# Softmax weights turned in 32x32 blocks: all pairs instead of every second, through one SBUF exchange

## What is computed

```python
q, k, v = (Q @ Wq + bq), (K @ Wk + bk), (V @ Wv + bv)        # layer 0, heads of 64; K = V = context
scores = einsum('bhqd,bhkd->bhqk', q, k) * scale
attn = softmax(where(attn_mask, -1e9, scores))
out = layernorm(einsum('bhqk,bhkd->bhqd', attn, v) @ Wo + bo + Q) * gamma + beta
...
x = layernorm(tgt + self_attention(tgt, tgt_mask) @ o_w)      # layer 1, heads of 16
x = layernorm(x + cross_attention(x, memory) @ co_w)
x = layernorm(x + relu(x @ lin1_w) @ lin2_w)
```

## Time and profile before

| | us |
|---|---|
| median of three runs | 1821.75 |
| the profiled execution | 1826.15 |
| its span | 1824.3 |
| PE / DVE / ACT / POOL busy | 1719.5 / 1269.6 / 1190.3 / 990.9 |
| DMA traffic | 324.12 MB in 227521 packets |

### The profile page before, as it was taken

One profiled execution on the slowest core, in us unless ns is written; L12 is line 12 of the kernel. 1 busy time (PEld: TensorE's weight loads), 2 busy tenths in 40 slices (PEclk: granted clock), 3 DMA queues, 4 the chain that ended last, 5 costly groups with the idle time before them and its releaser, 6 DMA issues.

```text
span 1824.3 us, 36986 instructions
## 1 busy us (share of the span) xinstructions
PE 1719.5 (94%) x11328; PEld 1287.7 (71%) x11328; DVE 1269.6 (70%) x4778; ACT 1190.3 (65%) x3985; POOL 990.9 (54%) x1030
## 2 busy tenths in 40 slices
PE   7999999999999999999999999999999999998887
PEld 5776677777777677777777777677777777776556
DVE  3465667786868668686776868678686867667763
ACT  3364766667676666767666676766667677566752
POOL 3252655657465464746556474555657565455742
PEclk9999999999999999999999999999999999998899
DMA  7432327585766758576585757658575766613010
GB/s 167 143 106 84 107 67 230 172 273 161 238 204 200 245 170 272 161 244 206 178 266 181 249 159 236 209 181 280 173 251 163 226 223 182 202 59 139 30 58 12
DMA packets 227521, 324.12 MB, mean 178 GB/s; under 512 B 31744, under 2 KB 196352, under 8 KB 219136
## 3 DMA queue, kind: packets, MB, share of 16 engines
q1 hardware_dynamic: 224208, 321.75, 55.5%
q10 hardware_dynamic: 3120, 0.01, 0.1%
HBM read 170.69 MB, written 151.00 MB: 176 GB/s over the span
## 4 chain that ended last, share of the span: by engine, by line
PE 77%; DVE 6%; DMA 5%; ACT 5%; SPq 5%; issue 2%; POOL 0%; POOLq 0%; DVEq 0%
PE ps_g L681 45%; PE ps_t L824 10%; PE ps_t L847 8%; PE ps_s L800 8%; ACT prob L930 3%; PE ps_av L800 3%; DMA prob_b<-p_kept 3%; PE ps_av L847 3%; DVE prob L1105 2%; DMA p_kept<-blocks 2%; SPq L593 1%; PE ps_g L687 1%; DVE res_ln L1081 1%; DVE prob_b L1136 1%; SPq L576 1%
## 5 line engine op out<-in xcount | busy, mean ns | idle before, releaser
L1229 POOL TENSOR_TENSOR prob<-prob,recip 128x512 f32<-128x512 f32 x768 | 788.4, 1049 | 670.5 <-DVE recip L1115 670.4
L930 ACT ACTIVATE prob<-prob,ext 128x256 f32<-128x256 f32 x1536 | 757.2, 499 | 11.7 <-DVE ext L1105 11.5
L940 ACT ACTIVATE prob_t<-ps_t 128x512 f32<-128x512 f32 x384 | 226.3, 594 | 398.1 <-PE ps_t L824 397.3
L824 PE MATMUL ps_t<-ident,prob 128*128 128x128 f32 x1920 | 304.6, 283 | 7.6 <-DVE prob_b L1136 5.4
L930 ACT ACTIVATION_READ_ACCUMULATOR prob<-prob,ext 128x1 f32 x1536 | 295.5, 192 | 0.0
L824 PEld LDWEIGHTS ps_t<-ident,prob 128*128 128x128 f32 x1920 | 216.9, 142 | 94.2 <-issue 51.6
L1105 DVE CUSTOM_DVE_ANT_0 prob<-ps_s,mask_a 128x256 f32<-128x256 f32 x392 | 145.3, 421 | 88.3 <-PE ps_s L800 70.6
L1127 DVE STREAM_TRANSPOSE blocks<-prob 128x512 f32<-128x512 f32 x288 | 183.9, 676 | 3.2 <-POOL prob L1229 2.3
L1105 DVE CUSTOM_DVE_ANT_0 prob<-ps_s,zero 128x256 f32<-128x256 f32 x392 | 144.4, 418 | 45.3 <-PE ps_av L800 37.3
L1105 DVE CUSTOM_DVE_ANT_0 prob<-ps_s,mask_b 128x256 f32<-128x256 f32 x368 | 135.9, 417 | 24.5 <-PE ps_s L800 14.8
L800 PE MATMUL ps_s<-k_ctx,q 64*128 64x256 f32 x784 | 144.8, 402 | 7.3 <-DVE ext L1105 3.0
(11 more groups left out here) (116 smaller groups left out, 2980.9 us busy)
## 6 DMA issues: line engine op xcount, KB each, us to landing
p_kept<-blocks SPq DMA_DIRECT2D x576, 128.0 KB, 2.4
prob_b<-p_kept SPq DMA_DIRECT2D x144, 512.0 KB, 3.4
k_parts_C<-k_hl SPq DMA_DIRECT2D x64, 256.0 KB, 3.1
k_parts_B<-k_hl SPq DMA_DIRECT2D x64, 256.0 KB, 3.1
q_parts_B<-q_hl SPq DMA_DIRECT2D x64, 256.0 KB, 3.5
k_B<-k_parts_B SPq DMA_DIRECT2D x16, 1024.0 KB, 7.6
q_B<-q_parts_B SPq DMA_DIRECT2D x16, 1024.0 KB, 7.7
q_parts_C<-k_hl SPq DMA_DIRECT2D x64, 256.0 KB, 4.7
```

The costliest lines, as they stand in the source:

```text
L824: last = nc.tensor.transpose(two(ps_t[e])[:, kt, qt * P:(qt + 1) * P], src[:, e, qt, kt * P:(kt + 1) * P], ident[:, :])
L930: last = nc.scalar.activation(tile, tile, ACT.Exp, bias=ext[:, slot, e, t:t + 1], scale=-1.0, accum_out=sums[:, slot, e, t:t + 1])
L940: nc.scalar.activation(prob_t[:, e], two(ps_t[e]), ACT.Copy).then_inc(copied_second, 1)
L1229: nc.gpsimd.tensor_tensor(rows, rows, recip[:, slot, e].unsqueeze(2) .to_broadcast([P, TT, TOK]), ALU.mult).then_inc(normed[s], 1)
```

## The change

- The odd pairs are turned on DVE too, in all bodies, and with one instruction of 128x1024 a pair. `T0`, `T1`, `L`, `turn`, `evac_turned` (on DVE and ACT) and `prob_t` are gone, and so is `p_kept`.
- `exchange` takes the place of `spill` and `load_back`: SP issues four transfers of 128 KB from `blocks` straight into `prob_b` for each pair, in the place in which it was turned. `prob_b` holds three quads (`T_RING`), `blocks` two (`B_RING`), `prob` three pairs (`P_RING`, from four). `turn_blocks` waits, for the even pair of a quad, until both pairs of the quad two before have landed; `exchange` until the quad three before was weighed.
- The exchange puts key r*4+g on the partition where the token's own order would have g*32+r. So scores have their key columns in that order: the host gives `ctx_keys` (and both masks) with permuted columns, a new input tile `c_k` feeds the key projections, and `keys_out` reads `x1_t` in that order for `ks`.
- `LAG` is 4 instead of 3: `weigh` comes five places behind the odd pair's scores.
- The banks freed: scores have four of their own (`ps_s`), `weigh` has `ps_av`; PE may start a pair's scores when the pair two before has been masked.
- B's keys and both queries are spread from SBUF to SBUF, eight issues of 128 KB each, without DRAM; the queries' on ACT, in two halves. C's keys still go through DRAM.
- ACT takes `v` instead of DVE. `x` is loaded straight into `res["ln0"]`, to which POOL adds the bias in place. The jobs stand at other places of the list.
- Weights and biases of layer 1 are arranged on the host and come in a few large transfers; POOL's `sort_weights` is gone.

```diff
-P_RING = 4
-LAG, BLOCKS = 3, 2
-BLOCKED = {(s, q) for s in "ABC" for q in range(QUADS)}
+P_RING, B_RING, T_RING = 3, 2, 3
+LAG, BLOCKS = 4, 2
-DVE_JOBS = {"q": 4, "v": 4, "kc": 1, "wo": 1,
+DVE_JOBS = {"q": 4, "kc": 1, "wo": 1,
-ACT_JOBS = {"k": 4, "vc": 1, "x1T": 1, "x2T": 1, "x3T": 1, "h": 3}
+ACT_JOBS = {"k": 4, "v": 4, "vc": 1, "x1T": 1, "x2T": 1, "x3T": 1, "h": 3}
...
             zip("AAABBCACBBCC", (0, 1, 2, 0, 1, 0, 3, 1, 2, 3, 2, 3)) for j in range(2)]
...
+        ("A", 0): [job("k", 2)],
+        ("A", 1): late + [job("ks")],
+        ("A", 2): [job("qs"), dma("k", "B"), ln("ln1")],
+        ("A", 3): [job("x2T"), job("q", 2), dma("q0", "B")],
+        ("A", 4): [job("qc"), dma("q1", "B")],
+        ("A", 5): [job("oc"), job("vs")],
+        ("B", 0): [ln("ln2"), io("value_c"), dma("q0", "C")],
+        ("B", 1): [job("x3T"), job("v", 2), dma("q1", "C"), res("res3", 0), res("res3", 1)],
+        ("B", 2): [job("h", 0)],
+        ("B", 3): [job("hd"), job("q", 3), res("res2", 0), res("res2", 1)],
+        ("C", 0): [job("k", 3), res("res1", 0)],
+        ("C", 1): [job("h", 1), job("h", 2), io("x_columns")],
+        ("A", 6): [job("v", 3), res("res1", 1)],
+        ("A", 7): [half("y")],
+        ("C", 2): [job("y"), io("x_in")],
+        ("C", 3): [io("mask_in"), job("kc"), job("vc")],
+        ("B", 4): [job("q", 0, "x")] * closed + [res("res0", 0)],
+        ("B", 5): [job("q", 1, "x")] * closed + [io("save_c"), io("c_columns"), ln("ln3")],
+        ("B", 6): [],
+        ("B", 7): [half("wo")] * closed + [io("store")],
+        ("C", 4): [job("wo")] * closed,
+        ("C", 5): [job("k", 0, "x"), job("v", 0, "x")] * closed,
+        ("C", 6): [job("k", 1, "x"), ln("ln0")] * closed,
+        ("C", 7): [job("v", 1, "x")] * closed,
...
+            def exchange(body, step):
+                n, quad, j = body.place(step), body.quad(step), step[2] % 2
                 sp.wait_ge(flipped, n + 1)
+                if quad >= T_RING and j == 0:
+                    (_, s0, p0, _), b0 = body.pair_at(2 * (quad - T_RING))
+                    sp.wait_ge(weighed[s0], count(b0, QUADS, p0 // 2 + 1))
                 for q in range(4):
+                    sp.dma_start(prob_b[:, quad % T_RING, q, j],
+                                 blocks[q * SLOT:(q + 1) * SLOT, quad % B_RING, :, j]
+                                 ).then_inc(landed[quad % T_RING], 16)
...
+                for part in range(PARTS):
+                    for e in range(2):
+                        row = HALF * e + DH1 * part
+                        sp.dma_start(k4["B"][row:row + DH1].bitcast(F32), k_hl[:, part % 2, e]
+                                     ).then_inc(spread_k["B"], 16)
...
             def turn_blocks(body, step):
                 _, s, p, _ = step
+                quad = body.quad(step)
                 dve.wait_ge(normed[s], count(body.batch(step), HEADS, 2 * p + 2))
+                if quad >= B_RING and p % 2 == 0:
+                    dve.wait_ge(landed[(quad - B_RING) % T_RING], 128 * ((quad - B_RING) // T_RING + 1))
+                src = prob[:, body.slot(step, P_RING)].rearrange("p e t (k g r) -> p (e t k) g r", k=TT, r=SLOT)
+                out = blocks[:, quad % B_RING, :, p % 2].rearrange("p g (m q) -> p m g q", q=SLOT)
+                nc.vector.transpose(out, src).then_inc(flipped, 1)
...
+                past = body.earlier(step, 2, lambda x: x[0] == "S")
                 if past:
                     (_, s0, p0, _), b0 = past
+                    pe.wait_ge(masked[s0], count(b0, HEADS, 2 * p0 + 2))
...
+            def spread_queries(body, step):
+                _, what, s, _ = step
+                b, half = body.batch(step), int(what[1])
...
+                act.wait_ge((q_high[s], taken["qs" if s == "B" else "qc"])[half], count(b, 1, 1))
+                for part in (2 * half, 2 * half + 1):
+                    for e in range(2):
+                        row = HALF * e + DH1 * part
+                        act.dma_start(q4[home][row:row + DH1].bitcast(F32), parts[:, half, e]
+                                      ).then_inc(spread_q[s], 16)
...
+                pe.wait_ge(landed[n % T_RING], 128 * (n // T_RING + 1))
+                by_query = [prob_b[:, n % T_RING, :, j].rearrange("p q (e t k r) -> p e k t q r", e=2, t=TT, k=TT)
+                            for j in range(2)]
```

More of the change, by code:

```diff
@@ L156, in schedule @@
     }
     if present == {"x", "a"}:
[L160 to L164, removed]
+        moved = ("res0", 0), ("x_in", 0), ("mask_in", 0), ("v", 2), ("v", 3), ("c_columns", 0)
+        after = {place: [x for x in jobs if x[1:3] not in moved] for place, jobs in after.items()}
@@ L165, in schedule @@
+        after["A", 7] = [job("v", 2)]
+        head += [res("res0", 0), io("mask_in")]
     steps += here(head)
-    line = Line(steps, carried, blocked)
+    line = Line(steps, carried)
     for o in order:
@@ L173, in schedule, with last_schedule @@
     if not closed:
-        for _ in range(LAG + 1):
-            line.advance([])
+        for i in range(LAG + 1):
+            line.advance([job("v", 3), io("c_columns")] if present == {"x", "a"} and i == 1 else [])
         steps += here(wo + os + first)
     return steps
-def last_schedule(carried, blocked):
+def last_schedule(carried):
     steps = []
@@ L550, in load_values @@
                              v_kept[bass.ds(b, 1)].rearrange("b p t d -> p b t d")).then_inc(v_loaded, 16)
-            def save_keys(body, step):
-                b = body.batch(step)
-                sp.wait_ge(taken["ks"], count(b, 1, 1))
-                if not (isinstance(b, int) and b == 0):
-                    sp.wait_ge(spread_k["B"], count(b - 1, 16, 16))
-                for part in range(PARTS):
-                    sp.dma_start(k_parts["B"][0, :, part].rearrange("e r c t -> (r c) e t"),
-                                 k_hl[:, part % 2]).then_inc(k_saved["B"], 16)
@@ L584, in spill, with spread_keys @@
-            def spill(body, step):
-                _, s, p, _ = step
-                n = body.turned_so(body.quad(step), True)
+                elif not (isinstance(b, int) and b == 0):
+                    sp.wait_ge(scored[s], count(b - 1, HEADS, HEADS))
+            def spread_keys(b):
+                sp.wait_ge(taken["ks"], count(b, 1, 1))
+                home_free("B", b, "B")
+                for part in range(PARTS):
+                    for e in range(2):
+                        row = HALF * e + DH1 * part
+                        sp.dma_start(k4["B"][row:row + DH1].bitcast(F32), k_hl[:, part % 2, e]
+                                     ).then_inc(spread_k["B"], 16)
@@ L932, in exps @@
                     last.then_inc(exped[s], 1)
-            def evac_turned(body, step, e):
-                if step[2] % 2 == 0:
-                    return
-                quad = body.quad(step)
-                act.wait_ge(turned, 2 * (quad + body.turned_so(quad + 1, False)) + e + 1)
-                nc.scalar.activation(prob_t[:, e], two(ps_t[e]), ACT.Copy).then_inc(copied_second, 1)
             def evac_weighed(body, step):
@@ L1095, in extremes @@
                 slot = body.slot(step, P_RING)
+                n = body.place(step)
+                if n >= P_RING:
+                    dve.wait_ge(flipped, n - P_RING + 1)
                 if s == "A" and p == 0:
```

532 lines of the change are left out of this document (198 added, 334 removed).

## The result

The changed kernel takes 2090.95 us (median of 4, 2088.70 to 2099.21) where the kernel before takes 1821.38 beside it: a ratio of 1.1475, 95% interval 1.1447 to 1.1504. The forecast was 1665 us, range 1605 to 1740. The profiled span is 2088.9 us, 264.6 more than before.

The account below looks back on a forecast made before the run. The prediction took PE, busy 94%, as the bound. Twelve full bodies falling from 106.9 to 97 us gave 119, the short bodies 10, 9 and 3, the last 20: 161 off 1826, forecast 1665 us, range 1605 to 1740.

Parts of the forecast that it names:

- the sign of being wrong: Body over 101 us with DVE and PE under 88%, L1127 waits for DMA, or SP back to back.
- Part 1, PE loses its transposes: Odd pairs' 96 transposes a body leave PE: 103.4 us falls to 88.3 to 92.9, taken as 91.
- Part 2, the round trip leaves the chain: Direct exchange into `prob_b` removes the DRAM wait, 9.0 us a body of the chain, but no second gain.
- Rival (e): B's keys spread at length over 16 partitions, so `scores` waits; chance 0.07 together with (d) and (f).
- Part 3, the transposes: DVE turns every pair at 1.12 us per 1024 columns: 89.2 us a body, as much as PE has left.
- Rival (f): DVE transposes and POOL lock each other out: up to 2.2 us each, DVE 115 us a body; chance 0.01.
- Part 4, ACT and SP: Per body, ACT falls from 74.1 to 71 us; SP issues take 60 to 65, exchange slack 11.
- rival (d): SP issues too slow, deciding from about 0.85 us each: 1900 us; chance 0.07 together with (e) and (f).
- How two nearly equal engines add up: PE and DVE work summed by groups of three to four places gives 97.5 us a body; 97 taken.
- Rival (c), the clock: PE's idle stops lower its clock, adding some 8 us a body: 105 us, 1780 in all; chance 0.06.

Follow-up runs that it names:

- before, context first: The kernel before with one edit, on ScalarE a weighed quad's context evacuated ahead of the place's exponentials: 1801.75 us beside 1823.58, ratio 0.9881.
- after, context first: The changed kernel with one edit, on ScalarE a weighed quad's context evacuated ahead of the place's exponentials: 2022.62 us.
- wide spreads: The changed kernel with each spread transfer of B's keys and both queries going to 128 partitions instead of 16 (keys and queries wrongly placed): 1921.25 us.
- keys through DRAM: The changed kernel with B's keys alone sent through DRAM again, queries still direct to 16 partitions on ACT: 1947.05 us.
- same, context first: The kernel with only B's keys through DRAM, plus the context evacuated ahead of the exponentials on ScalarE: 1871.92 us.
- wide, context first: The kernel with spreads to 128 partitions, plus the context evacuated ahead of the exponentials on ScalarE: 1843.62 us, ratio 1.0091.
- same, half transposes: The kernel with spreads to 128 partitions and the context first, plus each DVE transpose cut to half its columns: 1791.06 us.

## Why the prediction was wrong

A body of each kernel in us, PE's time at full clock, what the lower clock adds to it (half of its busy time at that level), and its idle time:

| kernel | body | PE at full clock | lower clock | idle |
|---|---|---|---|---|
| before | 106.9 | 102.5 | 0.9 | 3.5 |
| before, context first | 104.8 | 102.8 | 0.0 | 2.0 |
| forecast | 97 | 91 | 0 | 6 |
| after | 124.4 | 93.8 | 6.3 | 24.3 |
| after, context first | 119.3 | 93.9 | 4.5 | 20.9 |
| wide spreads | 112.8 | 93.9 | 6.0 | 13.0 |
| keys through DRAM | 113.1 | 93.9 | 4.7 | 14.5 |
| same, context first | 107.1 | 94.0 | 1.9 | 11.1 |
| wide, context first | 106.0 | 93.9 | 2.9 | 9.2 |
| same, half transposes | 103.4 | 93.9 | 2.1 | 7.4 |

PE's own work is the same 93.8 to 94.0 us in all versions of the changed kernel shown here; what differs is idle time and the lower clock behind it. The forecast missed by 27.4 us a body: 2.8 in PE's work, 6.3 in the clock, 18.3 in idle time. Twelve bodies make 329 of the 426 us by which it missed; the last body makes 43, the short ones 49, and some 5 lie outside. What I had named as the sign of being wrong is what came: a body over 101 us with PE (81%) and DVE (71%) both under 88%.

- *Part 1, PE loses its transposes.* The mechanism held, the size was off: 102.5 to 93.8 is 8.7 us, where I took 12.4 and had 10.5 as the least. The strided reads of `weigh` cost nothing, as I took. That of `keys_out`, which I put at nothing with 1.8 us as its bound, costs 1.9. The job `ks` in the changed kernel, then the same job before, eight records each, both at a granted clock of 1.00:

```profile
551.70 3.78 PE L606 MATMUL ps_g<-x_t,w_l 128*128 128x256 f32 x8
```

```profile
483.79 1.89 PE L681 MATMUL ps_g<-x_t,w_k 128*128 128x256 f32 x8
```

  It takes twice as long. The 10.5 us of transposes less these 1.9 are the 8.7 measured, to 0.1 us.
- *Part 2, the round trip leaves the chain.* For the probabilities this held: the exchange lands in 2.8 us in the median (at most 15.4, where I had 7.2), and in the ten bodies no matmul waits more than 0.3 us for it. The step that failed is its last sentence, where "B's keys and both queries skip DRAM" stood as a saving by bytes, with no price for the new transfers. I had no row for a transfer to 16 partitions and gave it no bounds, though I bounded the exchange. Nor did I follow who reuses its source: `k_hl` is wanted again by the split of C's queries at 943.5 us, 6.5 us after the first of the eight is issued, with `ctx_C` behind it. That step costs 11.3 to 13.3 us a body, the largest term. Rival (e) had B's keys spread "at length over 16 partitions so that `scores` waits": the right transfer with the wrong waiter, at 0.07 together with others. The port rule of the Trainium skill cited above gives an estimate of some 10 us for eight such transfers, and I had not weighed it. By itself it would not have given the cost: in the kernel before the same eight cost nothing.
- *Part 3, the transposes.* Held. From one of 1024 to the start of the next instruction it is 1.14 to 1.27 us (I had 1.12, at most 1.20 in the same measure). Their durations, 384 in a narrow band beside POOL, are below; DVE is busy 88.0 us a body (89.2). Rival (f) is refuted by it.

```profile
L1025 DVE STREAM_TRANSPOSE blocks<-prob x384: 1204/1215/1246, 28.4 to 2047.7; 128x1024 f32<-128x1024 f32 x192
```

- *Part 4, ACT and SP.* ACT is busy 64.8 us a body without its DMA issues (62 by my sum), and sends its queries at 0.63 us an issue in the median, 11.0 us a body (9). SP is busy issuing 72.6 us a body (60 to 65): the 117 issues are as many as I had, at 0.62 us each, not 0.52. That is below the 0.85 from which rival (d) would decide. In full bodies it doesn't. In the second short body SP does hold PE up: exchanges queue behind its other transfers and waits, as I had described it. SP, then PE:

```profile
150.24 2.38 SPq L507 DMA_DIRECT2D k_parts<-k_hl  x4
152.65 0.86 SPq L510 DMA_DIRECT2D v_kept<-c_k  x1
153.69 0.76 SPq L493 DMA_DIRECT2D c_t<-ctx_cols  x1
156.30 0.37 SPq L495 DMA_DIRECT2D c_k<-ctx_keys  x1
156.77 8.37 SPq L554 DMA_DIRECT2D prob_b<-blocks  x13
```

```profile
164.19 1.93 PE L744 MATMUL ps_av<-prob_b,v_B 128*32 128x256 f32 x16 [7.93 <-DMA prob_b<-blocks]
```

  Thirteen exchanges go out back to back once the saves and loads are through, and PE waits 7.93 us. I had forecast 9 us of gain here; it is 18 of loss.
- *How two nearly equal engines add up.* This asked for the wrong thing. Summing work by place assumes that an engine is late only when it has more work there. The two large stops are chains: an item that is ready but queued behind one that waits, on DVE (`ctx_C`) or on ACT (`k_ctx`, 5.3 us). The second of these is in the kernel before as 1.7 us. That it grew because PE's own work no longer covers it is how I read it; no run shows this apart from the new order of jobs. I named the releasers of today's stops and not what stands behind each wait in the queue.
- *Rival (c), the clock,* was of the right kind, at 8 us a body against 6.3 measured; but it came with the stops, not in their place.

Settled: narrow target and reuse of `k_hl`, and the context's place in ACT's order, together 18.4 us a body (124.4 to 106.0). Left in the body of 106.0 are 9.2 us idle (A5 2.7, B1 2.3, A3 2.2, rest below 1) on chains of norm, split and projection; swapping jobs didn't take such stops away, and what would is open. The last body, with its tail, takes 274.6 us before, 297.8 after, 282.0 with wide spreads and 278.7 with the context first too, so the same two causes hold most of its 23 us; halved transposes take 14 more there (264.6). The second short body stays at 101 us in both wide kernels (86.4 before, 104.0 after); no run was made for it.

## What to carry to other kernels

Give every transfer that changes its target's shape a price of its own, and look up who writes its source next: a copy that leaves DRAM out can hold its buffer longer than the copy through DRAM did. Where an engine works in order, list for each wait what stands behind it and is already ready; moving that ahead of the wait (here an evacuation ahead of exponentials) gave 22 us in the old kernel and 68 to 78 in the new ones. Taking work from the engine that bounds may also take away the cover of chains beside it (argued here, not shown), so a forecast should go through the stops that are short today, and not only through the sums. A read that changes its stride needs a price too: step four instead of one doubled a projection.

## What the runs showed of the hardware

- Eight transfers of 128 KB, SBUF to SBUF, to 16 partitions each take 10.7 us alone, to 128 partitions 6.5, issuing included; in the kernel, with eight more from ACT at the same time, their median landing is 9.0 us against 2.9 for wide ones, and in the stop at A5 the DMA engines show as full at 161 GB/s.
- A stop of PE costs more than its length: after 14.4 us the granted clock stayed at 0.50 for 3.39 us of full work. Over ten bodies the lower level added 6.3 us to a body with 24.3 us idle, 6.0 to one with 13.0 (wide spreads), and nothing in the kernel before with the context first (2.0 us idle, longest stop 1.50).
- DVE transposes 128x1024 in 1.215 us, 128x512 in 0.674: 0.54 us for 512 more columns.
- A float32 projection whose moving operand is read with a step of four elements takes 3.78 us for eight records, with a step of one 1.89 (128x256, granted clock 1.00).
